# A small weights' product as fp16 pairs: what twelve short fp16 matmuls in place of eight fp32 passes do to a graph-network kernel

## What is computed

```python
h = jnp.maximum(_layernorm(x, axis=-1), 0.0)
fv = h.mean(axis=1); nf = fv / norm(fv)
_, idx = top_k(nf[:, :, None] * nf[:, None, :], 9)      # idx[..., 1:] are the neighbours
A = symmetric 0/1 matrix of those neighbours, with ones on the diagonal
def _gc(x, A, W, b):
    return (A / A.sum(axis=2)) @ (x @ W.T + b)
h = relu(_gc(h^T, A, adj, b1)); h = _gc(h, A, adj, b2)
out = x + h^T
```

## Time and profile before

| | us |
|---|---|
| median of the three runs | 468.46 |
| lowest and highest | 467.45, 469.01 |
| the profiled execution, its own time | 466.62 |
| its span, first to last instruction | 464.8 |
| TensorE busy in the span | 421.0 |
| VectorE busy | 395.5 |
| ScalarE busy | 307.8 |
| GpSimd busy | 223.0 |

### The profile page before, as it was taken

The page is one execution under the profiler, slowest core; times in us unless marked ns, Lnnn a source line. Parts: engine busy times, 40 slices in busy tenths (PEclk is TensorE's granted clock), DMA queues, the critical chain, the costliest instruction groups (busy, mean ns, idle before and its releaser), DMA issues.

```text
span 464.8 us, 7615 instructions
## 1 busy us (share of the span) xinstructions
PE 421.0 (91%) x2220; PEld 176.1 (38%) x2220; DVE 395.5 (85%) x682; ACT 307.8 (66%) x657; POOL 223.0 (48%) x937
## 2 busy tenths in 40 slices
PE   0663899998989999899999999999999999999996
PEld 0121343334333444344444444444434444444432
DVE  5999898978999999999999999999999848844463
ACT  3979687969787799657967888677965752014300
POOL 2526656373838338624646373744565343315200
PEclk9995999999999999999999999999999999999999
DMA  8991000068404590076504590069304400430026
GB/s 308 362 411 56 1 0 1 36 237 276 179 0 186 189 352 0 2 271 229 223 3 181 185 359 1 29 245 322 131 0 183 182 1 0 183 157 25 0 104 259
DMA packets 19401, 68.21 MB, mean 147 GB/s; under 512 B 1824, under 2 KB 2464, under 8 KB 19360
## 3 DMA queue, kind: packets, MB, share of 16 engines
q1 hardware_dynamic: 19360, 67.73, 39.2%
HBM read 34.17 MB, written 33.55 MB: 146 GB/s over the span
## 4 chain that ended last, share of the span: by engine, by line
PE 42%; DVE 30%; ACT 12%; POOL 7%; issue 7%; DMA 1%; SPq 0%; POOLq 0%; DVEq 0%
PE ps L451 34%; DVE xs L1166 7%; DVE hl L1141 7%; DVE bn L1119 5%; ACT hl L677 4%; ACT hf L656 4%; ACT hl L665 3%; PE ps L457 3%; DVE hl L1150 3%; PE pm L506 2%; POOL nw L890 1%; DVE idx L1190 1%; DVE fv L1182 1%; PE pm L493 1%; PE pm L526 1%
## 5 line engine op out<-in xcount | busy, mean ns | idle before, releaser
L451 PE MATMUL ps<-hl,wh 128*128 128x512 f16 x896 | 268.7, 382 | 15.3 <-DVE wl L1325 11.3
L451 PE MATMUL ps<-hl,wl 128*128 128x512 f16 x448 | 170.6, 381 | 0.0
L451 PEld LDWEIGHTS ps<-hl,wh 128*128 128x128 f16 x896 | 83.7, 99 | 125.7 <-issue 22.0
L656 ACT ACTIVATE hf<-xs,nbias,rstd 128x1024 f32<-128x1024 f32 x64 | 79.2, 1237 | 24.6 <-POOL nbias L894 23.3
L1166 DVE SCALAR_TENSOR_TENSOR xs<-ps,sc,xs 128x1024 f32<-128x1024 f32 (+1 forms) x71 | 79.2, 1138 | 7.9 <-PE ps L457 7.9
L1141 DVE TENSOR_TENSOR hl<-hf,hl 128x1024 f16<-128x1024 f32 x64 | 77.3, 1211 | 6.8 <-ACT hl L665 6.6
L1150 DVE SCALAR_TENSOR_TENSOR hl<-ps,hl 128x1024 f16<-128x1024 f32 (+1 forms) x55 | 57.3, 1081 | 20.3 <-ACT hl L677 20.2
L677 ACT ACTIVATE hl<-ps 128x512 f16<-128x512 f32 x96 | 55.6, 593 | 22.4 <-PE ps L457 22.4
L665 ACT ACTIVATE hl<-hf 128x1024 f16<-128x1024 f32 x64 | 67.6, 1056 | 2.0
L908 POOL COPY gat<-hl 128x4 f16 x256 | 49.5, 245 | 32.7 <-DVE idx L1190 25.1
L1119 DVE BATCH_NORM_STATS2 bn<-xs 128x6 f32<-128x512 f32 x96 | 61.2, 677 | 4.4 <-DMA xs<-x_dram 4.3
(11 more groups left out here) (146 smaller groups left out, 523.2 us busy)
## 6 DMA issues: line engine op xcount, KB each, us to landing
xs<-x_dram SPq DMA_DIRECT2D x62, 512.0 KB, 7.4
out_dram<-xs SPq DMA_DIRECT2D x31, 1024.0 KB, 5.1
xs<-x_dram SPq DMA_DIRECT2D x4, 256.0 KB, 3.5
out_dram<-xs SPq DMA_DIRECT2D x4, 256.0 KB, 2.1
wt<-adj_t_dram SPq DMA_DIRECT2D x1, 256.0 KB, 10.5
b1r<-b_row_dram SPq DMA_DIRECT2D x1, 128.0 KB, 10.6
b2r<-b_row_dram SPq DMA_DIRECT2D x1, 128.0 KB, 11.4
cs<-consts_dram SPq DMA_DIRECT2D x1, 84.5 KB, 10.1
```

The lines of the kernel that those rows point to most:

```text
L451: pe.matmul(bank(i, e), w[:, k, o], src, start=(k == 0 and w is wh and part == 0), stop=False)
L656: act.activation(hf[:, c % NHF], xs[:, n % NX, k], ACT.Relu, bias=nbias[:, n % RB, k:k + 1], scale=rstd[:, n % RB, k:k + 1], accum_out=s_a ...
```

## The change

The class vectors are split into two fp16 parts, `q1h[:, 0]` (rounded) and `q1h[:, 1]` (the rest), by two more instructions on GpSimd at the end of `class_q1`. `times_q1` multiplies them with `wh` and `wl` in the three products of a pair, twelve matmuls for each group where there were four calls on fp32 (eight records in the trace). The result carries the factor S, which `class_values` takes away with a per-partition scale. TensorE waits for the two parts in place of the four writes of `q1`.

```diff
+        q1h = sb("q1h", [P, 2, KC, 64], F16)
...
+        q1h_ready = sem("q1h_ready")
...
             def times_q1(g):
-                pe.wait_ge(q1_ready, 4 * (g + 1))
+                pe.wait_ge(q1h_ready, 2 * (g + 1))
                 pe.wait_ge(nd_ready, g + 1)
                 pe.wait_ge(row_x, 2 * g + 1)
                 for m in range(KC):
                     for k in range(KC):
-                        last = pe.matmul(pm_q[:, m], wt[:, k, m * P:(m + 1) * P], q1[:, k],
-                                         start=(k == 0), stop=(k == KC - 1))
+                        for part, w in ((0, wh), (1, wh), (0, wl)):
+                            last = pe.matmul(pm_q[:, m], w[:, k, m * P:(m + 1) * P], q1h[:, part, k],
+                                             start=(k == 0 and part == 0 and w is wh), stop=(k == KC - 1 and w is wl))
                 last.then_inc(wq1_ready, 1)
...
-                    act.activation(v1[:, g % 2, m], pm_q[:, m], ACT.Relu, bias=b1[:, m:m + 1]
+                    act.activation(v1[:, g % 2, m], pm_q[:, m], ACT.Relu, bias=b1[:, m:m + 1], scale=scal(S_I)
                                    ).then_inc(v1_ready, 1)
...
                 pool.tensor_tensor(q1[:, :, 32:64].rearrange("p k (b u) -> p k b u", b=GB), q1u[:],
                                    rdeg[:, s, :, 4:5].unsqueeze(1).to_broadcast(full), ALU.mult
                                    ).then_inc(q1_ready, 1)
+                pool.wait_ge(q1_ready, 4 * (g + 1))
+                pool.tensor_copy(q1h[:, 0], q1[:]).then_inc(q1h_ready, 1)
+                pool.wait_ge(q1h_ready, 2 * g + 1)
+                pool.tensor_tensor(q1h[:, 1], q1[:], q1h[:, 0], ALU.subtract).then_inc(q1h_ready, 1)
```

## The result

The changed kernel takes 466.79 us, the median of 20 runs (465.59 to 468.20), against 468.54 us for 20 runs of the kernel before. The ratio is 0.9957, with a 95% interval of 0.9944 to 0.9970: 2.0 us faster, between 1.4 and 2.6 (the two medians lie 1.75 apart). The forecast was 468.0 us against a base of 468.46, 0.5 us faster, inside what can be told from no change. The time lies in the stated range, but the change did more than forecast: rival A (466.6 us) comes nearest.

The account below looks back on a forecast made before the run. The prediction took TensorE's `times_q1` to set the time in groups 1, 2, 6 and 7, other engines' chain in 3 to 5. TensorE -0.8, late VectorE +0.1, scale +0.2 gave -0.5: 468.0 us against 468.46, range 466.3 to 470.0.

Parts of the forecast that it names:

- rival A: TensorE's products come at the pace of their columns, every 0.0275 us: 466.6 us, faster; chance 0.20.
- The place of the gain in the last groups: `times_q1` on TensorE sets the time in groups 6 and 7, 0.21 us gained each; groups 3 to 5 give nothing.
- The distance of the products: In `times_q1` on TensorE, a product every 0.056 us: twelve take 0.67 us, 0.21 less than 0.88.
- the sign of being wrong: For `times_q1` on TensorE, a distance between products below 0.035 or above 0.096 us would make the prediction wrong.
- The figure of 81 ns a pair: Trainium skill's pace for weight load and 128-column matmul: twelve take 0.97 us on TensorE, four groups 0.4 us slower.
- Four groups on the chain: TensorE's `times_q1` stands in the chain in groups 1, 2, 6 and 7: 4 x 0.21 = 0.8 us gained.
- The stall of group 0: GpSimd's subtraction waits under a VectorE operation, TensorE waits some 0.8 us, and later idle time absorbs the delay.
- the idle 0.86 us named for it: TensorE's idle time before 74.17 us, in which the rest of group 0's delay was to disappear.
- the pair: GpSimd's added cast (0.30 us) and subtraction (0.43) cost 0.9 us with waits, hidden behind TensorE's `main` in groups 1 to 7.
- The 0.1 us for a late L1141: In group 0 VectorE's L1141 can start up to 0.1 us later behind the cast; 0.1 entered the sum.
- The scale: ScalarE's per-partition scale costs about 0.10 us an activation, two a group; 0.2 us counted in group 0 alone.
- The sum: Whole kernel: -0.8 + 0.1 + 0.2 = -0.5 us, giving 468.0 us against 468.46.

Follow-up runs that it names:

- experiment 3: Changed kernel with the fp32 products and a scale of ones in groups 3 to 5 alone; 466.58 us, ratio 0.9967 to the kernel before.
- experiment 4: Changed kernel with the fp32 products and a scale of ones in groups 6 and 7 alone; 467.63 us, ratio 0.9984 to the kernel before.
- Experiment 7: Changed kernel with the fp32 products and a scale of ones in groups 1 and 2 alone; 467.16 us, ratio 0.9966 to the kernel before.
- experiment 1: Changed kernel with the split kept but fp32 products and a scale of ones in all groups; 468.28 us against 468.25 for the kernel before.
- experiment 2: Changed kernel without the two split instructions: GpSimd writes the fp16 high part, the low part is zero; 466.64 us, ratio 0.9966 to the kernel before.
- experiment 6: Changed kernel with two GpSimd operations moved behind the split, making it 0.7 us earlier; 466.72 us against 468.77 for the kernel before.
- experiment 5: Changed kernel without the per-partition scale on ScalarE, the division by S left out; 466.80 us against 468.77 for the kernel before.
- experiment 8: Changed kernel with the factor S left in the class values, no ScalarE scale, and the split earlier; 467.45 us against 468.77 for the kernel before.
- experiment 11: Changed kernel with the factor S left in the class values and no ScalarE scale, split unmoved; 466.59 us against 468.15 for the kernel before.
- experiment 9: The changed kernel run once more, unaltered, for a second profile; 465.92 us, one time.

## Why the prediction was right or wrong

**The place of the gain in the last groups: right.** The 0.58 us reach the end in group 6 (50.60 to 50.01) and group 7 (47.66 to 47.07), and nothing comes from groups 3 to 5 (experiments 3 and 4).

**The distance of the products: mis-sized.** This is the step that made the forecast too small. The prediction took 0.056 us between two products, by the proportion of the fp32 loads, and bounded it by 0.0275 from below. Measured is 0.030, a hair above the lower bound and below the 0.035 that the prediction itself had named as the sign of being wrong. So twelve products take 0.36 us and not 0.67. The fp32 product took 0.94 up to the `main` behind it and not 0.88, and the difference is 0.58 us a group and not 0.21. The load of 128 columns still lasts 0.098 us, and yet a new one begins every 0.030: about three are under way at a time, where the fp32 loads (0.192 long, every 0.11) had shown not quite two. The proportion taken from them did not carry over. With 0.030 the prediction's own sum would have been 4 x 0.52 (0.88 less 0.36) - 0.3, some 1.8 us faster.

The figure of 81 ns a pair, from the Trainium skill's "TensorE: Matmul & The Clock Gate", section "Back-to-back issue gap", is for 128 columns. Here, at 64 columns and a granted clock of 1.00 (2.4 GHz), the trace has 30 ns, and the rule that spoke against the change does not carry over. The prediction had worked out a time from it, 0.4 us slower, without giving it a chance of its own. The table in that section of the Trainium skill gives about 60 cycles for up to 64 columns, an estimated 25 ns at 2.4 GHz; the measured 30 is near that.

**Four groups on the chain: wrong for two.** In groups 1 and 2 a second chain through ScalarE and VectorE lies close under TensorE's. Group 2 gave 0.23 us of 0.58, and group 1 at most 0.07 (its stretch grew by 0.10 with a scale that costs 0.17). Experiment 7 shows it from the other side. The step that failed is the reading of a place in the chain as its full value: the prediction asked whether TensorE is on the chain, and not how far the next chain lies behind. The two errors, a size too small and a count too large, partly cancel: 2 x 0.58 + 0.23 + 0.07 = 1.5 us where 0.8 was forecast. The stated range, 466.3 to 470.0, is wide enough to hold the sum with either error put right alone (466.7 with the size, 468.3 with the count), so the time lying in it says little for the mechanism.

**The stall of group 0: right but for a term of 0.1 us.** The cast lasted 0.289 (predicted 0.30), the subtraction 0.428 (0.43) and 1.45 in group 0, TensorE waited 0.70 (0.8), and the wait was gone at the idle 0.86 us named for it (experiments 1, 2 and 6). In groups 1 to 7 the pair took 0.29 and 0.43 us and TensorE waited nowhere. The 0.1 us for a late L1141 did not come: it lasts 1.22 as before.

**The scale: right in size, short in count.** One activation grew by 0.092 us (0.10 predicted). It was counted in group 0 alone; group 1 pays it too, since with the short product the chain there passes through ScalarE. That is 0.35 us instead of 0.2.

**The sum.** 1.5 gained less 0.35 is 1.1 us, plus 0.3 where the tie of group 5 falls well: the traces account for 1.1 to 1.5 us. The times say 1.4 to 2.6 in the 20 runs, and the other variants with the fp16 products in groups 6 and 7 (experiments 2, 3, 5 to 8 and 11) lie between 1.5 and 2.8 by their middle values. The two accounts meet only at their edge.

A part of the rest lies in executions that no profile shows. Of the 98 runs of the kernel before in all these comparisons, 33 took more than 469 us, up to 470.68. Of the 96 runs of kernels with fp16 products in groups 1 and 2 (the change and experiments 2 to 6, 8, 9 and 11), none took more than 468.43. With the fp32 products everywhere (experiment 1) it is 3 of 12, and with fp32 in groups 1 and 2 alone (experiment 7) 4 of 12. Without its runs above 469 the kernel before has a median of 468.09, 1.3 us over the 466.79 of the change, and that is what the traces account for. So the short product in groups 1 and 2 seems to keep the kernel out of a longer course that costs it about 2 us in a third of its executions. The 469 was chosen after seeing the times. What takes longer in such an execution stays open, since the longest of the thirteen profiled ones took 467.46 us. The time before the first class degrees is no likely explanation: the first `main` begins at 42.82 to 44.96 us in the ten profiles with fp16 products, and at 42.56 to 43.12 in the three without.

## What to carry to other kernels

Duration is not distance: for a form that the trace does not show, give the pace of its columns a good chance when loads already run ahead of products; here the distance came out at 0.030 us against 0.0275 by columns and 0.098 by the load. Before counting a step that stands on the chain at full value, look at how close the second chain is; an experiment that makes the step longer in one group alone settles it, and so does the distance between two instructions, which here repeats within 0.1 us where the times of whole executions scatter over 4. But look at the spread of the times as well as at one profile: an execution of the kind that no profile caught can hold a part of the gain. A stall is only worth what is left of it at the next wait.

## What was not expected of the hardware

Whether one small GpSimd operation cost 0.2 us or 1.3 hung on a few nanoseconds: it began 39 to 41 ns ahead of a VectorE operation with two inputs from SBUF, or 29 to 38 ns. This holds for that one instruction. In the first profile of the change the same line, for an earlier batch, began at 12.91 us, 39 ns ahead as well, and was caught for 1.29 us. Begun 0.05 ahead, a longer operation (0.43 us) made VectorE's wait instead, 1.45 us in place of 1.22 (experiment 11). Shortening GpSimd's work can thus lengthen VectorE's.
